# New constants for a schedule planner, and the first feed-forward weights asked for without waiting for the last attention stacks

## The reference

```python
x = x + xattn(layernorm(x), ctx, ctx, mask, Wq, bq, Wk, bk, Wv, bv, Wo, bo)   # 16 heads of 32
x = x + ffn(layernorm(x), Ws, bs, W1, b1, W2, b2)

# xattn: softmax(q k^T * 32**-0.5, masked) v, heads joined, @ Wo + bo
# ffn: expert choice, 8 experts; each takes the k = 4096/8 = 512 tokens it likes best
route_prob = softmax(xf @ Ws + bs).T
route_vals, routes = top_k(route_prob, 512)
h = gelu(einsum('ekd,edf->ekf', xf[routes], W1) + b1)        # F = 2048
out = (einsum('ekf,efd->ekd', h, W2) + b2) * route_vals[..., None]
final = zeros.at[routes].add(out)
```

## Time and profile before

| | |
|---|---|
| median of three runs | 1667.03 us (1666.02 to 1667.8) |
| the profiled execution, its own time | 1667.8 us |
| its span, from the first instruction to the last | 1666.0 us |
| mean granted TensorE clock | 0.985 of full speed |
| TensorE busy | 1597.9 us (96%) |
| VectorE, ScalarE, GpSimd busy | 1113.7, 976.8, 300.0 us |
| attention (about) | 0 to 893 us |
| experts (about) | 930 to 1666 us |

### The profile page before, as it was taken

One profiled execution on the slowest core, in us unless ns is written; L12 is line 12 of the kernel. 1 busy time (PEld: TensorE's weight loads), 2 busy tenths in 40 slices (PEclk: granted clock), 3 DMA queues, 4 the chain that ended last, 5 costly groups with the idle time before them and its releaser, 6 DMA issues.

```text
span 1666.0 us, 22367 instructions
## 1 busy us (share of the span) xinstructions
PE 1597.9 (96%) x7847; PEld 1162.0 (70%) x7847; DVE 1113.7 (67%) x1950; ACT 976.8 (59%) x2115; POOL 300.0 (18%) x396
## 2 busy tenths in 40 slices
PE   7999999999999999999886999999999999999997
PEld 5556666666666666666544787888888888888885
DVE  7676878878788797787746577765554555454543
ACT  5788898989989899798872223222222223232331
POOL 6220221302213022130300201002020202020110
PEclk9999999999999999999997999999999999999999
DMA  5643654626547364462611423416252524343330
GB/s 179 184 123 95 193 145 140 208 80 205 144 132 207 87 200 147 134 192 83 190 67 64 127 89 90 152 57 184 76 159 101 159 91 144 101 132 119 102 110 26
DMA packets 131271, 217.27 MB, mean 130 GB/s; under 512 B 17116, under 2 KB 51056, under 8 KB 131160
## 3 DMA queue, kind: packets, MB, share of 16 engines
q1 hardware_dynamic: 114520, 173.23, 33.1%
q0 software_dynamic: 16640, 42.61, 9.6%
HBM read 157.45 MB, written 57.82 MB: 129 GB/s over the span
## 4 chain that ended last, share of the span: by engine, by line
PE 86%; DVE 7%; ACT 2%; DMA 2%; issue 2%; POOL 0%; SPq 0%; DVEq 0%; POOLq 0%; ACTq 0%
PE ps_gen L888 9%; PE ps_gen L890 9%; PE ps_gen L889 9%; PE ps_gen L1905 7%; PE ps_gen L2069 7%; PE ps_gen L2071 7%; PE ps_gen L2070 7%; PE ps_gen L1873 7%; PE ps_att L1916 7%; PE ps_gen L1855 3%; PE ps_gen L1856 3%; PE ps_gen L1857 3%; PE ps_gen L1932 2%; PE ps_gen L1933 2%; PE ps_gen L1934 2%
## 5 line engine op out<-in xcount | busy, mean ns | idle before, releaser
L1476 DVE TENSOR_REDUCE nmax<-ps_gen 128x1 f32<-128x512 f32 x512 | 331.9, 684 | 79.5 <-PE ps_gen L1873 77.8
L1292 ACT ACTIVATE p_ring<-ps_gen,keep_scale 128x512 f32<-128x512 f32 x512 | 341.3, 702 | 44.2 <-PE ps_gen L1905 30.7
L1280 ACT ACTIVATE ps_gen<-ps_gen,nmax 128x512 f32<-128x512 f32 x512 | 342.6, 676 | 33.6 <-DVE nmax L1476 33.4
L1349 ACT ACTIVATE gel<-ps_gen,b_cols 128x512 f32<-128x512 f32 x128 | 88.3, 690 | 448.8 <-PE ps_gen L890 448.7
L1737 DVE TENSOR_TENSOR gel_lo<-gel,gel_hi 128x512 fp32r<-128x512 f32 x126 | 87.3, 692 | 281.6 <-ACT gel_hi L1350 277.3
L888 PE MATMUL ps_gen<-hT_hi,w_hi 128*128 128x512 f32 x512 | 202.2, 395 | 0.2 <-DVE hT_lo L1730 0.2
L1873 PE MATMUL ps_gen<-kst,qst 97*128 97x512 f32 x512 | 193.0, 424 | 8.6 <-issue 4.6
L890 PE MATMUL ps_gen<-hT_hi,w_lo 128*128 128x512 f32 x512 | 199.5, 390 | 0.0
L889 PE MATMUL ps_gen<-hT_lo,w_hi 128*128 128x512 f32 x512 | 199.4, 389 | 0.0
L1905 PE MATMUL ps_gen<-qst,kst 99*128 99x512 f32 x512 | 194.9, 424 | 3.8 <-DMA qst<-by_row 3.1
L2069 PE MATMUL ps_gen<-w_hi,gel_hi 128*128 128x512 f32 x504 | 198.1, 393 | 0.0
(11 more groups left out here) (218 smaller groups left out, 2672.0 us busy)
## 6 DMA issues: line engine op xcount, KB each, us to landing
w_raw<-in_L_ffn_W SPq DMA_DIRECT2D x128, 512.0 KB, 3.3
kst<-qk_rows SPq DMA_DIRECT2D x93, 256.0 KB, 4.0
qst<-qk_rows SPq DMA_DIRECT2D x93, 256.0 KB, 4.1
x_in<-in_x POOLq DMA_DIRECT2D x60, 256.0 KB, 4.1
out_x<-x_in SPq DMA_DIRECT2D x32, 256.0 KB, 3.3
qk_rows<-kT_hi SPq DMA_DIRECT2D x31, 256.0 KB, 2.3
qk_rows<-kT_lo SPq DMA_DIRECT2D x31, 256.0 KB, 3.7
qk_rows<-qT_hi SPq DMA_DIRECT2D x31, 256.0 KB, 2.0
```

The source lines that it names most:

```text
L1280: e.activation(psum[:, :], psum[:, :], ACT.Exp, bias=nmax[g % 2][:, c], scale=-1.0, accum_out=den[g % 2][:, c]).then_inc(drained_sem("max" ...
L1292: e.activation(p_ring[n % NP_][:, :], ps("score", g, kt, h)[:, :], ACT.Exp, scale=keep_scale[:, b:b + 1]).then_inc(drained_sem("score", g, ...
L1476: e.tensor_reduce(nmax[g % 2][:, h * TB + t:h * TB + t + 1], ps("max", g, h, t)[:, :], AX.X, ALU.min).then_inc(s_min, 1)
```

## The change

The diff has two parts. The first gives the planner other numbers: slightly shorter costs of TensorE's steps, a shorter cost of `rows_lo` (2.60 for 3.20 until its result is seen), a smaller `LOOK`, and other due times throughout. The second takes the stacks of group 31 and its `rows_lo` out of the needs of `piece_in` and makes its due time 30 instead of 31. No instruction is added or removed; which instructions stand before which on each engine, and which PSUM bank each step takes, follow from the plan.

```diff
 COST = {
-    "pe": {"proj": (0.700, 0.90), "max": (0.235, 0.43), "rows": (0.109, 0.31), "rden": (0.436, 0.63), "score": (0.235, 0.43),
-           "att": (1.120, 1.17), "v": (2.78, 2.98), "turn": (0.436, 0.63), "outa": (1.395, 1.60), "osum": (0.700, 0.90),
-           "out": (1.395, 1.60), "route": (0.436, 0.63), "logits": (0.405, 0.52), "back": (0.109, 0.31)},
+    "pe": {"proj": (0.693, 0.89), "max": (0.231, 0.43), "rows": (0.109, 0.31), "rden": (0.436, 0.63), "score": (0.231, 0.43),
+           "att": (1.105, 1.15), "v": (2.74, 2.94), "turn": (0.436, 0.63), "outa": (1.386, 1.59), "osum": (0.693, 0.89),
+           "out": (1.386, 1.59), "route": (0.436, 0.63), "logits": (0.405, 0.52), "back": (0.109, 0.31)},
...
-    "pool": {"rows_lo": (1.050, 3.20), "recip": (0.560, 0.66), "load": (0.550, 4.00), "load_wo": (0.550, 3.30),
+    "pool": {"rows_lo": (1.050, 2.60), "recip": (0.560, 0.66), "load": (0.550, 4.00), "load_wo": (0.550, 3.30),
...
-LOOK = 0.048
+LOOK = 0.023
...
-K_AT = ((0.297, 0.404), (-0.045, 0.294), (0.028, 0.08), (-0.316, 0.132))
-Q_AT = ((0.442, 0.479), (0.235, 0.318), (0.087, 0.372), (0.259, 0.437))
-MAX_AT = ((-0.075, 0.651), (-0.033, 0.729), (-0.086, 0.786), (0.287, 0.737))
-ROWS_AT, RECIP_AT, RDEN_AT, OSPLIT_AT, ATT_AT = -0.391, 0.334, 1.071, -0.392, 0.061
+K_AT = ((0.24, 0.248), (-0.055, 0.281), (0.094, 0.256), (-0.698, -0.096))
+Q_AT = ((0.472, 0.472), (0.34, 0.351), (0.109, 0.318), (0.248, 0.412))
+MAX_AT = ((0.124, 0.67), (0.036, 0.694), (-0.083, 0.753), (0.309, 0.742))
+ROWS_AT, RECIP_AT, RDEN_AT, OSPLIT_AT, ATT_AT = 0.132, 0.197, 0.833, -0.55, 0.042
...
     done = [("pe", "proj", w, NG - 1, DC - 1) for w in "kq"] + [("pe", "v", B - 1, TB - 1)]
-    stacked = [("sync", "stack_" + k, w, NG - 1) for k in ("hi", "lo") for w in "kq"] + [("pool", "rows_lo", NG - 1)]
     for n in range(3):
-        p.add("sync", ("piece_in", n), NG - 1, done + stacked)
+        p.add("sync", ("piece_in", n), NG - 2, done)
     p.add("pool", ("tables",), NG - 2, done)
```

More of the change, by code:

```diff
@@ L369 @@
 }
-LOOK = 0.048
+LOOK = 0.023
 HELD = {"max": 3, "score": 2}
 LAG = {
[L373 to L379, removed]
-}
@@ L381 @@
-K_AT = ((0.297, 0.404), (-0.045, 0.294), (0.028, 0.08), (-0.316, 0.132))
-Q_AT = ((0.442, 0.479), (0.235, 0.318), (0.087, 0.372), (0.259, 0.437))
-MAX_AT = ((-0.075, 0.651), (-0.033, 0.729), (-0.086, 0.786), (0.287, 0.737))
-ROWS_AT, RECIP_AT, RDEN_AT, OSPLIT_AT, ATT_AT = -0.391, 0.334, 1.071, -0.392, 0.061
+    ("act", "proj"): 0.065, ("dve", "proj_lo"): 0.032, ("pool", "rows_lo"): -0.605, ("act", "rows"): -0.136, ("dve", "rows_lo"): -0.141,
+    ("sync", "stack_hi"): -0.046, ("sync", "stack_lo"): 0.395, ("pool", "recip"): 0.043, ("dve", "rden"): -0.186, ("dve", "outa"): -0.4,
@@ new lines @@
+    ("dve", "csplit_lo"): -0.274, ("dve", "turn_lo"): 0.082, ("dve", "v"): 0.188, ("dve", "out"): 0.019, ("act", "turn"): 0.006,
+    ("dve", "back"): -0.047, ("act", "osplit"): -0.275, ("dve", "divide"): 0.345, ("act", "logits"): -0.091, ("pool", "add_bias"): -0.545,
+    ("act", "csplit"): -0.079, ("pe", "rows"): 0.166, ("dve", "route"): -0.071, ("dve", "max"): -0.081, ("dve", "recip"): -0.034,
+    ("act", "score"): 0.027, ("act", "sum"): 0.034, ("pe", "score"): -0.219, ("dve", "osplit_lo"): 0.15,
+}
@@ L385 @@
+K_AT = ((0.24, 0.248), (-0.055, 0.281), (0.094, 0.256), (-0.698, -0.096))
+Q_AT = ((0.472, 0.472), (0.34, 0.351), (0.109, 0.318), (0.248, 0.412))
+MAX_AT = ((0.124, 0.67), (0.036, 0.694), (-0.083, 0.753), (0.309, 0.742))
+ROWS_AT, RECIP_AT, RDEN_AT, OSPLIT_AT, ATT_AT = 0.132, 0.197, 0.833, -0.55, 0.042
 SPAN = {
-    "v": (-1, 0.205, 1.615), "load_c": (-3, -0.376, 0.177), "csplit": (-3, -0.778, -0.281), "load_x": (-3, 0.705, 0.812),
-    "stats": (-3, 0.598, 0.608), "norm": (-3, 0.591, 1.147), "turn": (-3, 0.372, 0.504), "residual": (2, -0.162, 0.443),
@@ L388 @@
-    "add_bias": (2, 1.633, 2.372), "outa": (2, 0.177, 1.039), "out": (4, 0.057, 0.784), "x1_norm": (4, 0.602, 1.176),
-    "route": (4, 0.403, 1.087), "logits": (4, 0.556, 1.139), "back": (4, 0.744, 1.133),
+    "v": (-1, 0.295, 1.594), "load_c": (-3, -0.536, 0.13), "csplit": (-3, -0.167, -0.092), "load_x": (-3, 0.752, 0.887),
+    "stats": (-3, 0.587, 0.597), "norm": (-3, 0.577, 0.856), "turn": (-3, 0.676, 0.826), "residual": (2, -0.159, 0.515),
+    "add_bias": (2, 1.445, 2.219), "outa": (2, 0.138, 0.992), "out": (4, 0.006, 0.738), "x1_norm": (4, 0.603, 1.647),
@@ L390 @@
+    "route": (4, 0.389, 1.208), "logits": (4, 0.608, 1.2), "back": (4, 0.751, 1.343),
 }
```

## The result

The changed kernel takes 1691.24 us (median of 4 runs, 1683.93 to 1697.06), the kernel before 1667.41 us on the same chips. The ratio is 1.0132 with a 95% interval of 1.0109 to 1.0153: it is slower by 1.3%, some 22 us. (The ratio fits the 24 executions of the changed kernel on record, whose median is 1689.5 us.) The forecast was 1671 us with a range up to 1681. The sign was right; the size was not. The profiled execution of the changed kernel took 1688.73 us; its span is 1686.9 us, 20.9 us more than before. Its lines have numbers smaller by 2: L1871 is `max`, L1903 `score`, L900 and L902 the pieces.

What follows compares the result with a forecast made beforehand. The prediction took TensorE, 86% of the chain, to bound the kernel. It summed 1667.8 + 4.6 - 1.0 = 1671.4 us, or 1670.6 us from the median, and said 1671 us, range 1658 to 1681 us.

Steps and rivals of the forecast that it cites:

- The place of the pieces: On SyncE at group 31: all three pieces come ahead of q's stacks, the first ones ahead of its stores.
- Term A: At group 31: early pieces delay q's last stack, so `max` starts later; +4.6 us, bounds 0 and +8.6 us.
- rival four: At group 31: pieces hold SyncE's queue strictly, q's last stack lands 8.6 us later; 1674.6 us, chance 0.09.
- Term B: In TensorE's order: new costs and due times give -3.0 + 2.0 = -1.0 us, bounds -14.4 and +14 us.
- rival three: In the batches: retuned order loses, maxima rows taken as seen too early, q's stacks late; 1678.4 us, chance 0.13.
- The steps on the costs: In the planner's table: 2.60 us for `rows_lo` right for most groups, costing 2.0 us; shorter TensorE costs taken as nothing.

Runs made afterwards that it cites:

- numbers_only: The changed kernel with the old needs and due time of `piece_in`: 1682.54 us against 1670.97 us for the kernel before, ratio 1.0065.
- norows pair: Kernel before, and changed kernel with old `piece_in`, both with `score` leaving out the maxima rows: 1663.46 and 1673.99 us, against 1671.01 us; one run each.
- pe_only: The kernel before with only TensorE's row of costs made about 1% shorter: ratio 1.0253 to the kernel before.
- numbers_rows320: The changed kernel with the old `piece_in` and `rows_lo` back at 3.20 us: ratio 1.0073 to the kernel before.
- due_only: The kernel before with the new `LOOK`, `LAG`, due times and `SPAN`, but old costs and old `piece_in`: ratio 1.0177 to the kernel before.
- rows260_only: The kernel before with only `rows_lo` changed from 3.20 to 2.60 us: ratio 1.0112 to the kernel before.
- pieces_late: The kernel before, with SyncE waiting for the landing of group 31's maxima rows before asking for the first piece: ratio 0.9988.

## Why the prediction was wrong

**The place of the pieces: right.** SyncE's timeline shows them ahead of q's stacks and partly ahead of its stores, as worked out, and numbers_only takes the gap away. That the early landing gains nothing was right too: the experts take 734.4 us in both.

**Term A: the mechanism right, the size off.** It was +4.6 us; groups 29 to 30 grew by 8.9 us, 7.4 of it by the pieces (against numbers_only). I had let SyncE ask for the pieces from 823.44 on, computed one queue of 4.5 MB at 380 GB/s and added 1 to 3 us for round trips. The rows from 832 to 852 us sum to 5.5 MB at a mean of 275 GB/s: there was 1 MB more to move, and the engines were not full at either end of it. The stores of q sat in that traffic for 8.24 and 8.49 us, and only then could their stacks be issued, which took 8.50 and 6.40 us more. `max` of group 31 came 20.6 us after q's last projection, against 12.7 us in numbers_only: 7.9 us, where 4.6 was put. The upper bound of 8.6 us (rival four, with 0.09) was the nearest. That the work behind would run at the lower clock was foreseen, but not that this would last longer: 17 us between groups 28 and 30, against 7 before. In the old order, where I had worked it out, the same edit moved groups 29 to 30 by 6.4 us, and the median by 4.8.

**Term B: the step that failed.** The prediction said: "The only waits that this part can move are those listed." On that it took -3.0 + 2.0 = -1.0 us. numbers_only measures +0.65%, 11 us. The waits listed bound what a better order can gain, since TensorE's idle time can only be taken away once. They say nothing of what another order can lose. Its parts came out thus: the gain at the start is real and near its size (-3.9 us up to group 4, where 3.0 was put for two places together; from 60 to 80 us TensorE is idle for 1.8 us instead of 3.15); but the six batches lost 13.1 us, and the period of 103.3 us, whose change by more than 0.3 the prediction had named as its own sign of being wrong, became 105.1 to 105.6 us even at full clock. Of these 2.0 us and more a batch the wait for the maxima rows, which rival three had, is less than half (about 0.8 us, by the norows pair), the wait for `qT_lo` is 0.9 us by name, and both are waits that did not stand in the earlier trace rows in that size, or at all. On top come stretches at the lower clock, about 1.6 us each: one in the six batches of the changed kernel, three in those of numbers_only, one before. In the batches they had no term at all.

**The steps on the costs.** I took 2.60 us for `rows_lo` as right for most groups, by the row that shows a median of 1.7 us from issue to landing. The row was read rightly (the changed kernel has a median of 1.9 us), but the use was wrong: a truer number in the table does not give a better order. That number alone costs 1.1% in the kernel before, the 1% shorter costs of TensorE alone 2.5%, both together 0.56%. For the latter I had "no row for what that does, and take nothing"; that was the largest single effect in the study.

**Why.** What is shown: each change of these numbers reshuffles the order of a batch, the result repeats in every batch, and it comes to stand at another wait each time (stacks in pe_only, the maxima rows and q's bank in numbers_only, ScalarE in numbers_rows320). In part it is worse in the plan itself (due_only by 1.7 us a batch, rows260_only by 1.3), in part only on the chip. What is argued: the numbers before fit one another, and any step away from them falls among orders of which most are worse. The six other sets of numbers run here give mean batches of 105.4 to 111.3 us, and none reaches the 103.9 of the kernel before; that is in favour, but six are few. The planner's own period, which could have been had before any run, gives the changed order as 0.2 us a batch longer: the right sign, and a tenth of the size.

**The range and the chances.** The bound of term B, +14 us, was written down and held the truth (+11); added to term A's bound it gives 1690 us. The range ended at 1681, as if the two could not both be bad.

## What to carry to other kernels

When a diff changes the inputs of a scheduler, the idle time before tells only what can be gained; put the loss side from the kinds of waits that the schedule keeps away at present, times the number of repetitions, for a wait of 0.5 us in each batch is multiplied by the batches. Ask the scheduler for its own period first, and compare batches at equal clock: a new wait can also bring a stretch at the lower clock behind it. Numbers of such a table belong together: trying them singly, or correcting one towards the measured time, can be worse than changing all. A large prefetch that is not needed for tens of microseconds is better held back until the last small transfers on a critical round trip are through (early it cost 0.29% here, held back nothing that could be seen), and moving it to another engine's queue does not do that.

## What was not expected of the hardware

- Three pieces of 1.05 MB each on GpSimd's queue delayed SyncE's round trip (store, then stack) as much as the same pieces in SyncE's own queue: 19.9 against 18.3 us from q's last projection to the first `max`, and 10.8 and 11.6 us in the same order without them in the way (pieces_late, before). Each is one execution.
- A 256 KB store that took 3.65 us behind other small ones took 8.24 us beside the pieces (834.72 to 842.96 us), while DMA moved 304 GB/s from 836 to 840 us and 367 from 840 to 844.
- A shorter ScalarE step (256 for 512 columns) made the batches of the old order longer, 104.6 for 103.9 us, at full clock, in one execution.
- TensorE's clock came down to 1.2 GHz for a short stretch in one of the changed kernel's six batches, at the end of a wait of 0.93 us, and that batch was about 1.6 us longer (106.7 for 105.1 us). In pe_only it came down in every batch, and at 436.1 us right behind a wait of 2.97 us.
